# Later places for the chunk operations of layer 2: 72 dense steps from closing to table write instead of 52

## The chip, the cores and the metric

The kernel runs as one program on one NeuronCore of a Trainium2 chip. The metric is device time in microseconds for the whole program. TensorE (PE) multiplies matrices, VectorE (DVE) and ScalarE (ACT) work elementwise, GpSimd (POOL) issues the gathers, SyncE (SP) issues the other transfers. Each engine executes its own list of instructions in order and waits for the others on semaphores.

## The reference, cut to what matters

A graph with N = 6250 nodes of 128 features and 106250 edges. Three graph convolutions, then an edge-message layer:

```python
def conv(x, W_l, b_l, W_r):
    agg = segment_sum(x[src], dst) / max(degree, 1)
    return agg @ W_l.T + b_l + x @ W_r.T
h  = relu(layernorm(x))
h1 = relu(conv(h, ...))              # layer 0 of the kernel
h2 = relu(conv(h1, ...)) + h1        # layer 1
x  = x + conv(h2, ...)               # layer 2
h  = relu(layernorm(x))
m  = silu(concat(h[src], edge_attr) @ mw1 + mb1)      # layer 3
x  = h + silu(concat(h, segment_sum(m, dst)) @ uw1 + ub1) @ uw2 + ub2 + x
```

## The kernel before, in words

Nodes are handled in 49 tiles of 128 rows (`NTILE`), and these in 13 chunks of four tiles (`NCH`; the last has one tile). The edges, sorted by destination, are split: the first 600 tiles of edges of layers 1 and 2 are summed *densely*, the rest by gathers.

**Dense steps.** Layer 2 has 490 of them (`STEPS[2]`: 10 rounds of 49). Step d multiplies the two halves of node tile d % 49 with a *unit*, 128x500 counts, and accumulates into a bank (`dense_step`, L1142, two matmuls). Units are counts that SP loads piece by piece (seven units each, a ring of three pieces) and that are cast to fp32r: six of seven by ACT, one by DVE (`turn_unit`, L560). There are seven unit buffers. An engine at step i of its list casts unit i + 4 (`TURN_AHEAD`), and a cast waits until PE has used the unit seven before.

**Blocks.** Between the steps, about every sixth, PE sums one *block* of gathered edges (`sum_block`, L1092), POOL gathers the rows for it (L844, three gathers a block, a ring of seven blocks), and DVE adds the block's sum to `acc` (L1582) and makes a later one-hot (L1572). In layer 2 the 77 blocks stand at steps 34, 39, 45 and so on up to 480. At the end of each round DVE drains the bank (L1593) and adds five groups to `acc` (L1608) at steps 2, 4, 6, 8 and 10 of the next round.

**Chunks.** A chunk of nodes *closes* when all its edges are in `acc`. `CLOSING` gives the steps: 108, 157, 205, 206, 255, 304, 334, 353, 451, 457 within the rounds, and 490, 492, 494 for the last three, behind them. These are k = 0 to 12 below. For each closed chunk the rest of layer 2 and the node part of layer 3 is done, each operation some steps behind the closing, between the dense steps of the engine that does it:

- DVE multiplies by the inverse degree (`chunk_average`, L1708) at +0; PE multiplies by the two weights (`chunk_convolve`, L1212, L1213) at +4; ACT adds the bias (`convolved`, L954, "z"); PE turns it (`chunk_turn`, L1221).
- DVE zeroes the sums (`chunk_zero`, L1715), adds the input x (`chunk_residual`, L1721), and takes mean and variance (L1724, L1729); ACT takes the deviation (`chunk_deviation`, L959); DVE makes scale and shift (`chunk_shift`, L1736, L1738); ACT normalises with four activations, one per tile (`normalised`, L967).
- PE turns that (`chunk_hn_turn`, L1230), ACT copies it (`chunk_features`, L973), DVE adds it to what is kept for the output (`chunk_keep`, L1751, L1753), PE multiplies by the message weights (`chunk_message`, L1239), DVE adds a bias (`chunk_bias`, L1745), SP writes the rows to table 3 (`write_row_table`, L607).

Each engine finds its part with `closing(i, lag)`: all chunks k with `CLOSING[k] + lag == i`. SP runs by pieces and has its own places: the load of x (`load_x`, L602) at +10, the table write at `TABLE_AT + 20`. Steps from 490 on are only an order: nothing dense is left there. Each of four kinds of PE product has one bank for all chunks but k = 11, so the same operation of the next chunk waits until ACT or DVE has read the bank. Table 3 must be written completely before layer 3 gathers from it.

Of the kernel before, what the change touches and what calls it, by code (L numbers as in the profile page):

```python
# [42 lines left out]
JC = 4  # L43
CH = JC * P
NCH = -(-NTILE // JC)
# [184 lines left out]
CLOSING = [closing_tick(c) for c in TURN]  # L230
ENDING = sum(1 for t in CLOSING if t < STEPS[2])
assert TURN[ENDING:] == [7, 8, 12] and all(t + 10 < STEPS[2] for t in CLOSING[:ENDING])
CONV_AT, ZERO_AT, TURN_AT, RESIDUAL_AT, SHIFT_AT, HN_TURN_AT, MESSAGE_AT, KEEP_AT, BIAS_AT, TABLE_AT = 4, 8, 9, 10, 12, 21, 27, 20, 28, 32


def closing(i, lag):

    return [k for k in range(NCH) if CLOSING[k] + lag == i]
# [25 lines left out]
def gnn_kernel(nc, x, src_t, src_row, dst_t, dst_first, tile_first, edge_T, WlT, bl, WrT, mw1, mb1, uw1, ub1, uw2, ub2, out):  # L264
    with ExitStack() as ctx:
# [259 lines left out]
        def chunk_at(k):  # L525
            c = TURN[k]
            return c, k % 2, JC if c < NCH - 1 else JL
# [325 lines left out]
        def _(act):  # L853
# [57 lines left out]
            for l in range(4):  # L911
                if l == 0:
                    act.wait_ge(prep, PREP_PLACES)
                    act.wait_ge(starts_ready, 1)

                    def places(k):
                        return act.value_load(place_row[0:1, k:k + 1], min_val=0, max_val=P ** BT - 1)

                    def place_of(t):
                        return act.snap(((three[t % GT // BT] >> (7 * (t % BT))) & (P - 1)).with_bounds(min_val=0, max_val=G - CW))  # L920

                    three = [places(k) for k in range(GT // BT)]
                    coming = []
                    at = place_of(0)
                    for t in range(NC):
                        g = t // GT
                        if t % GT == 0:
                            after(act, counts_out[g % 2], 16 * (g // 2))
                        act.wait_ge(tile_counted, t + 1)
                        counted = nc.scalar.copy(stage[:, g % 2, :, bass.ds(at, CW)], count_bank(t))  # L930
                        if t > 0:
                            counted._wait_ge(counts_ready, t)
                        counted.then_inc(counts_ready, 1)
                        if t % GT in PLACES_AT and g + 1 < NG:
                            coming.append(places((g + 1) * GT // BT + len(coming)))
                        if (t + 1) % GT == 0:
                            three, coming = coming, []
                        if t + 1 < NC:
                            at = place_of(t + 1)
                        normalise_chunks(t)  # L940
                        if t % GT == GT - 1:
                            act.wait_ge(counts_ready, t + 1)
                            act.dma_start(counts[g], stage[:, g % 2].rearrange("p h w -> p (h w)")).then_inc(counts_out[g % 2], 16)
                elif l == 1:
                    for d in range(TURN_AHEAD, STEPS[1]):
                        turn_step(1, d)
                elif l == 2:
                    s = st[3]

                    def convolved(k):  # L950
                        c, q, n = chunk_at(k)
                        act.wait_ge(s["z_mm"], k + 1)
                        after(act, s["turned"], k - 1)
                        nc.scalar.activation(z[:, q, 0:n * P], chunk_bank(0, k)[:, 0:n * P], ACT.Identity, bias=bcol[:, 2:3]).then_inc(s["z_ready"], 1)  # L954

                    def chunk_deviation(k):
                        c, q, n = chunk_at(k)
                        act.wait_ge(s["var_ready"], k + 1)
                        nc.scalar.activation(std[:, q, 0:n], meanvar[:, q, 0:n, 1], ACT.Sqrt, bias=eps_col[:, 0:1]).then_inc(s["std_ready"], 1)  # L959

                    def normalised(k):
                        c, q, n = chunk_at(k)
                        act.wait_ge(s["y_ready"], k + 1)
                        after(act, s["hn_turned"], k - 1)
                        after(act, s["h_added"], k - 1)
                        for j in range(n):
                            m = nc.scalar.activation(hn[:, q, j, :], kept(c, n)[:, j, :], ACT.Relu, scale=rstd[:, q, j:j + 1], bias=shift[:, q, j:j + 1])  # L967
                        m.then_inc(s["hn_ready"], 1)

                    def chunk_features(k):  # L970
                        c, q, n = chunk_at(k)
                        act.wait_ge(s["hn_turned"], k + 1)
                        nc.scalar.copy(hT[:, cols(c, n)], chunk_bank(2, k)[:, 0:n * P]).then_inc(s["hT_ready"], 1)  # L973

                    for i in range(CLOSING[-1] + MESSAGE_AT):
                        if i + TURN_AHEAD < STEPS[2]:
                            turn_step(2, i + TURN_AHEAD)
                        for k in closing(i, CONV_AT):
                            convolved(k)
                        for k in closing(i, RESIDUAL_AT):  # L980
                            chunk_deviation(k)
                        for k in closing(i, SHIFT_AT):
                            normalised(k)
                        for k in closing(i, HN_TURN_AT):
                            chunk_features(k)
                elif l == 3:
                    def node_share(c):
                        n = JC if c < NCH - 1 else JL
                        act.wait_ge(st[4]["z_mm"], c + 1)
                        nc.scalar.copy(hT[:, cols(c, n)], bank[2][:, 0:n * P]).then_inc(st[4]["z_ready"], 1)  # L990

                    def last_high_half(c):

                        n = JC if c < NCH - 1 else JL
                        act.wait_ge(st[2]["high_ready"], NCH + c + 1)
                        nc.scalar.copy(last_halves[:, c * JC:c * JC + n, 0, :], hn[:, c % 2, 0:n]).then_inc(st[2]["half0_ready"], 1)

                    def updated(c):

                        act.wait_ge(st[4]["z_added"], c + 1)  # L1000
                        to = hT[:, cols(c, JC if c < NCH - 1 else JL)]
                        nc.scalar.activation(to, to, ACT.Silu, bias=bcol[:, 3:4]).then_inc(st[4]["z_ready"], 1)

                    act.wait_ge(flag_ready, 1)
                    n_left = act.value_load(left_flag[0:1, 0:1], min_val=0, max_val=EP)
                    with act.If(n_left > 0):
                        s = lf[3]
                        with act.Fori(0, NT) as t:
                            act.wait_ge(s["pre"], t + 1)
                            nc.scalar.activation(msg_left, pre_left, ACT.Silu).then_inc(s["msg"], 1)  # L1010
                    act.wait_ge(unit_used, unit_number(2, STEPS[2]))
                    for n in range(NB + SILU_AT):
                        if 2 <= n < NCH + 2:
                            node_share(n - 2)
                        for c in updates(n, SILU_AT):
                            updated(c)
                        if n >= NB:
                            continue
                        if n < NCH:
                            last_high_half(n)  # L1020
                        for k in fetch_starting(n + 3):
                            after(act, source_hot_ready, NTILE * (k - 1))
                            act.wait_ge(source_row_in[k % 2], 16 * (k // 2) + 16)
                            nc.scalar.copy(source_f[:, k % 2], source_row[:, k % 2]).then_inc(source_f_ready, 1)
                        for k in fetch_starting(n - COPY_AFTER):
                            act.wait_ge(fetch_summed, k + 1)
                            after(act, edge_mm, FETCHED[k - 1] + 1 if k > 0 else 0)
                            nc.scalar.copy(turned_pre[:, :], bank[7][:, 0:BT * P]).then_inc(fetch_copied, 1)
                        act.wait_ge(pre_ready, n + 1)
                        nc.scalar.activation(msg[:, n % NMSG], msg[:, n % NMSG], ACT.Silu).then_inc(msg_ready, 1)  # L1030
                if l < 2:
                    s = st[l + 1]
# [890 lines left out]
```

## Time and profile before

| what | value |
|---|---|
| median of 3 runs | 2372.09 us (2362.65 to 2381.28) |
| profiled execution | 2367.98 us, its span 2366.2 us |
| granted TensorE clock, mean | 0.947 |
| PE busy | 2075.7 us (88%) |
| POOL busy | 1655.9 us (70%) |
| DVE busy | 1468.7 us (62%) |
| ACT busy | 1136.4 us (48%) |

Busy times are sums over the whole span; the stages differ. The dense steps of layer 1 lie between 657 and 962 us of the span, those of layer 2 between 1002 and 1344 us, and layer 3 begins with its first gather at 1377 us. The granted clock is a share of 2.4 GHz; the clock has two levels, 1.2 and 2.4 GHz, so a mean between 0.5 and 1 is a mixture. "Idle before" in a row is the time that the engine did nothing ahead of the instruction, with what ended it behind the arrow.

### The profile page before, as it was taken

What the parts mean: (1) busy time and instruction counts of PE and PEld (TensorE: products, weight loads), DVE (VectorE), ACT (ScalarE), POOL (GpSimd) and SP (SyncE); (2) the same over time, 40 slices, a digit from 0 to 9 for tenths busy, and PEclk for the clock granted to TensorE, in tenths of its full rate; (3) what the DMA queues carried; (4) which work ended last, traced back from release to release, by engine and by line L of the source; (5) the groups of instructions that cost most, each with busy time, mean ns of one, the idle gap of its engine ahead of it and who ended that gap; (6) DMA issues with size and microseconds to landing.
All of it is one profiled execution on the core that took longest, in us unless ns stands there. A gap on an engine that the chain in (4) does not pass through costs nothing.

```text
span 2366.2 us, 44471 instructions
## 1 busy us (share of the span) xinstructions
PE 2075.7 (88%) x13062; PEld 1633.0 (69%) x13062; DVE 1468.7 (62%) x4334; ACT 1136.4 (48%) x2077; POOL 1655.9 (70%) x1666
## 2 busy tenths in 40 slices
PE   1489999999799999899999879899989889999987
PEld 0235555444378777487777658889988888888876
DVE  8878778877533333634444457667676667676764
ACT  4777777766487777687677532111111111111111
POOL 4477777777377777577766157777777777777775
PEclk9689999999899999999999979999999999999997
DMA  4389999898588778487787544434444444444432
GB/s 124 113 284 310 294 307 308 298 298 284 184 249 278 249 246 257 121 285 245 229 250 236 167 139 121 116 109 123 123 113 118 114 123 113 114 119 117 119 108 54
DMA packets 270042, 447.23 MB, mean 189 GB/s; under 512 B 34148, under 2 KB 219815, under 8 KB 263143
## 3 DMA queue, kind: packets, MB, share of 16 engines
q1 hardware_dynamic: 206680, 267.00, 37.0%
q0 software_dynamic: 55920, 114.62, 16.8%
q10 hardware_dynamic: 7200, 62.72, 6.7%
q8 instruction: 109, 1.79, 0.3%
q14 instruction: 133, 1.09, 0.1%
HBM read 363.79 MB, written 80.42 MB: 188 GB/s over the span
## 4 chain that ended last, share of the span: by engine, by line
POOL 36%; PE 33%; issue 14%; DVE 9%; DMA 3%; ACT 2%; DVEq 1%; POOLq 0%; ACTq 0%
POOL gath L844 35%; PE bank L1142 13%; PE bank L1150 6%; PE bank L1092 4%; PE bank L1111 3%; DMA gath<-table,src_sb 3%; PE bank L1192 2%; DVE region L1627 1%; PE bank L1177 1%; PE bank L1095 1%; PE bank L1114 1%; PE bank L1212 1%; ACT shared L967 1%; PE bank L1239 1%; PE bank L1161 1%
## 5 line engine op out<-in xcount | busy, mean ns | idle before, releaser
L844 POOL DMA_INDIRECT gath<-table,src_sb x1572 | 1555.3, 989 | 499.4 <-issue 457.7
L1142 PE MATMUL bank<-unit,halves 128*128 128x500 f32 x1960 | 509.3, 407 | 17.6 <-ACT unit L560 12.5
L560 ACT CAST unit<-region 128x500 fp32r<-128x500 f16 x840 | 453.7, 606 | 106.3 <-PE bank L1142 103.2
L1030 ACT ACTIVATE msg<-msg 128x384 f32<-128x384 f32 x277 | 145.2, 524 | 733.9 <-DVE msg L1670 679.2
L1192 PE MATMUL bank<-source_hot,last_halves 128*128 128x384 f32 x2352 | 494.8, 356 | 0.0
L930 ACT CAST shared<-bank 128x490 f32 x600 | 373.8, 623 | 142.7 <-PE bank L1114 108.5
L1142 PEld LDWEIGHTS bank<-unit,halves 128*128 128x128 f32 x1960 | 362.0, 193 | 92.6 <-ACT unit L560 21.8
L1698 DVE TENSOR_SCALAR source_hot<-source_f,source_col 128x384 fp32r<-128x384 f32 x1176 | 422.6, 422 | 2.1 <-PE bank L1192 1.4
L1192 PEld LDWEIGHTS bank<-source_hot,last_halves 128*128 128x128 f32 x2352 | 414.5, 196 | 3.8 <-issue 2.9
L1582 DVE TENSOR_TENSOR acc<-acc,bank 128x31 f32 (+1 forms) x548 | 105.3, 192 | 371.3 <-PE bank L1092 254.1
L1150 PE MATMUL bank<-region,parts 128*128 128x500 f16 x1176 | 318.1, 378 | 10.1 <-DVE dense_sum L1593 10.1
L1092 PEld LDWEIGHTS bank<-onehot,msg 128*128 128x128 f32 x1662 | 231.3, 201 | 135.9 <-ACT msg L1030 129.3
L1092 PE MATMUL bank<-onehot,msg 128*128 128x31 f32 x1662 | 230.2, 276 | 95.4 <-ACT msg L1030 83.5
L1670 DVE TENSOR_TENSOR msg<-bank,gath 128x384 f32<-128x384 f32 x253 | 140.5, 555 | 245.9 <-issue 166.4
L1177 PE MATMUL bank<-mw,region 128*128 128x128 f32 x1518 | 242.5, 299 | 0.9 <-DVE shared L1745 0.9
L1111 PE MATMUL bank<-region 128*128 128x490 bf16 x600 | 220.2, 395 | 20.6 <-DVE region L1627 13.0
L1627 DVE TENSOR_SCALAR region<-iota_h,key 128x540 bf16<-128x540 f16 x600 | 216.0, 395 | 28.2 <-PE bank L1114 25.3
L1177 PEld LDWEIGHTS bank<-mw,region 128*128 128x128 f32 x1518 | 203.0, 203 | 7.0 <-issue 7.0
L1150 PEld LDWEIGHTS bank<-region,parts 128*128 128x128 bf16 x1176 | 90.9, 100 | 90.9 <-issue 13.0
L1092 PEld LDWEIGHTS bank<-onehot,gath 128*128 128x128 f32 x924 | 124.4, 191 | 38.4 <-issue 29.2
L1572 DVE TENSOR_TENSOR onehot<-iota_f,rel 128x93 f32<-128x93 f32 x548 | 136.5, 251 | 0.3 <-issue 0.2
L1111 PEld LDWEIGHTS bank<-region 128*128 128x128 bf16 x600 | 59.2, 99 | 106.1 <-DVE region L1627 27.7
(164 smaller groups left out, 1686.6 us busy)
## 6 DMA issues: line engine op xcount, KB each, us to landing
region<-counts SPq DMA_DIRECT2D x196, 875.0 KB
counts<-shared ACTq DMA_DIRECT2D x50, 1225.0 KB
region<-in_edge_T SPq DMA_DIRECT2D x138, 384.0 KB
gath<-table,src_sb POOLq DMA_INDIRECT x1572
table<-shared SPq DMA_DIRECT2D x36, 256.0 KB, 2.3
table<-parts SPq DMA_DIRECT2D x12, 384.0 KB, 2.6
source_row<-in_src_row SPq DMA_DIRECT2D x24, 192.0 KB, 3.7
acc<-in_x SPq DMA_DIRECT2D x12, 256.0 KB, 5.1
```

The source lines that it names most:

```text
L560: copy(units[h][:, :].rearrange("p (b n) -> p b n", b=RG), ring[:, q, :, h * G:(h + 1) * G]).then_inc(done, 1)
L844: pool.indirect_dma_start(out=(gath if l > 0 else gath_parts)[:, BT * place + j, :], out_offset=None, in_=table[l], in_offset=bass.Indirec ...
L930: counted = nc.scalar.copy(stage[:, g % 2, :, bass.ds(at, CW)], count_bank(t))
L1030: nc.scalar.activation(msg[:, n % NMSG], msg[:, n % NMSG], ACT.Silu).then_inc(msg_ready, 1)
L1092: mm = nc.tensor.matmul(summed_in(l, n)[:, 0:W], of, onehot[:, n % HOTS, j, :], start=(j == 0), stop=(j == BT - 1))
L1111: mm = nc.tensor.matmul(count_bank(t), low_of(t), pairhot[:, t % NPAIR, 0:KW].rearrange("p (h w) -> p h w", h=NTILE), start=True, stop=(t ...
L1142: mm = nc.tensor.matmul(sum_bank(ordinal), halves[:, hi, a, :], units[h][:, :], start=(hi == 0 and a == 0), stop=(hi == NTILE - 1 and a == 1))
L1150: mm = nc.tensor.matmul(sum_bank(ordinal)[:, 0:g * G].rearrange("p (b n) -> p b n", b=g), parts[:, hi, a, :], ring[:, q, 0:g, h * G:(h + 1 ...
L1177: mm = nc.tensor.matmul(edge_bank(n)[:, j * D:(j + 1) * D], efT[:, h % NEF, t * P:(t + 1) * P], mw[:, 1, :], start=True, stop=True)
L1192: mm = nc.tensor.matmul(bank[7][:, 0:BT * P], last_halves[:, h, a, :], source_hot[:, y % NHOT, :], start=(h == 0 and a == 0), stop=False)
L1627: nc.vector.tensor_scalar(pairhot[:, t % NPAIR, :], iota_h[:, :], key[:, t:t + 1], None, ALU.is_equal).then_inc(pairhot_ready, 1)
L1698: nc.vector.tensor_scalar(source_hot[:, y % NHOT, :], source_f[:, k % 2], source_col[:, h:h + 1], None, ALU.is_equal).then_inc(source_hot_ ...
```

## The change

The lags of the chunk operations in layer 2 are set anew, in steps behind the closing:

| operation | engine | before | after |
|---|---|---|---|
| average | DVE | 0 | 0 |
| convolve | PE | 4 | 4 |
| z | ACT | 4 | 8 |
| zero | DVE | 8 | 10 |
| turn | PE | 9 | 13 |
| residual, mean and variance | DVE | 10 | 15 |
| deviation | ACT | 10 | 21 |
| shift | DVE | 12 | 24 |
| normalise, tiles 0 and 1 | ACT | 12 | 27 |
| normalise, tiles 2 and 3 | ACT | 12 | 30 |
| second turn | PE | 21 | 36 |
| keep | DVE | 20 | 36 |
| feature copy | ACT | 21 | 40 |
| message | PE | 27 | 46 |
| bias | DVE | 28 | 48 |
| table write | SP | 52 | 72 |

The last three chunks (k = 10 to 12) still normalise all their tiles at one place, +27. `chunk_deviation` waits, from k = 2 on, for the scale of the chunk two before, which reads the same buffer. The functions of the other engines are the same and take the new constants.

```diff
-CONV_AT, ZERO_AT, TURN_AT, RESIDUAL_AT, SHIFT_AT, HN_TURN_AT, MESSAGE_AT, KEEP_AT, BIAS_AT, TABLE_AT = 4, 8, 9, 10, 12, 21, 27, 20, 28, 32
+CONV_AT, Z_AT, ZERO_AT, TURN_AT, RESIDUAL_AT, DEVIATION_BY, SHIFT_AT, HN_AT, HN_REST_AT = 4, 8, 10, 13, 15, 21, 24, 27, 30
+HN_TURN_AT, KEEP_AT, FEATURES_BY, MESSAGE_AT, BIAS_AT, TABLE_AT = 36, 36, 40, 46, 48, 52
...
                         act.wait_ge(s["var_ready"], k + 1)
+                        if k > 1:
+                            act.wait_ge(st[0]["rstd_ready"], NCH + k - 1)
...
-                    def normalised(k):
+                    def normalised(k, tiles):
...
-                        for j in range(n):
+                        for j in tiles:
                             m = nc.scalar.activation(hn[:, q, j, :], kept(c, n)[:, j, :], ACT.Relu, scale=rstd[:, q, j:j + 1], bias=shift[:, q, j:j + 1])
-                        m.then_inc(s["hn_ready"], 1)
+                        if tiles[-1] == n - 1:
+                            m.then_inc(s["hn_ready"], 1)
...
-                    for i in range(CLOSING[-1] + MESSAGE_AT):
+                    for i in range(CLOSING[-1] + FEATURES_BY + 1):
...
-                        for k in closing(i, CONV_AT):
+                        for k in closing(i, Z_AT):
                             convolved(k)
-                        for k in closing(i, RESIDUAL_AT):
+                        for k in closing(i, DEVIATION_BY):
                             chunk_deviation(k)
-                        for k in closing(i, SHIFT_AT):
-                            normalised(k)
-                        for k in closing(i, HN_TURN_AT):
+                        for k in closing(i, HN_AT):
+                            normalised(k, range(JC // 2) if k < ENDING else range(chunk_at(k)[2]))
+                        for k in closing(i, HN_REST_AT):
+                            if k < ENDING:
+                                normalised(k, range(JC // 2, JC))
+                        for k in closing(i, FEATURES_BY):
                             chunk_features(k)
```

## Rows read from the trace of the kernel before

**Rows 1.** The page's chain of work that ended last, by engine.
```profile
POOL 36%; PE 33%; issue 14%; DVE 9%; DMA 3%; ACT 2%; DVEq 1%; POOLq 0%; ACTq 0%
```
**Rows 2.** Stretches: length; busy PE, PEld, DVE, ACT, POOL; clock, DMA share, GB/s.
```profile
657.10:962.00 304.90, 284.90 (x1443) 237.18 (x1442) 97.07 (x317) 228.38 (x423) 221.87 (x234) 0.98 0.82 256
1001.50:1343.60 342.10, 323.90 (x1643) 263.41 (x1642) 149.11 (x476) 252.04 (x490) 223.26 (x234) 0.97 0.76 237
1343.60:1377.00 33.40, 18.29 (x62) 12.10 (x61) 15.47 (x53) 7.38 (x18) 0.18 (x1) 0.68 0.34 107
...
1150.00:1155.00 5.00, 3.84 (x14) 3.15 (x14) 1.39 (x3) 4.17 (x9) 3.78 (x5) 0.66 0.65 196
```
**Rows 3.** Timeline of PE, layer 2: first and last block, two undisturbed ones.
```profile
1022.18 0.75 PE L1092 MATMUL bank<-onehot,gath 128*128 128x31 f32 x6
...
1281.65 0.75 PE L1092 MATMUL bank<-onehot,gath 128*128 128x31 f32 x6
...
1311.69 0.75 PE L1092 MATMUL bank<-onehot,gath 128*128 128x31 f32 x6
...
1337.75 0.75 PE L1092 MATMUL bank<-onehot,gath 128*128 128x31 f32 x6
```
**Rows 4.** Groups by line, PE, 1000 to 1345 us: busy, mean, idle.
```profile
L1212 PE MATMUL bank<-acc,wl 128*128 128x512 f32 x20 | 10.7, 618 | 2.6 <-DVE acc L1708 2.5
L1239 PE MATMUL bank<-mw,hT 128*128 128x128 f32 x80 | 10.6, 275 | 0.7 <-DVE shared L1745 0.7
...
L1230 PE MATMUL bank<-ident,shared 128*128 128x128 f32 x40 | 6.1, 277 | 0.0
```
**Rows 5.** Waits, 1000 to 1345 us: total us, times, longest us.
```profile
ACT shared L954 <- PE bank L1213: 28.6, 10, 3.6
...
ACT std L959 <- DVE meanvar L1729: 19.6, 8, 3.7
...
PE bank L1142 <- ACT unit L560: 12.5, 13, 1.5
DVE acc L1608 <- DVE acc L1608: 9.5, 11, 0.9
...
PE bank L1239 <- DVE shared L1745: 0.7, 1, 0.7
PE bank L1221 <- DVE acc L1721: 0.7, 1, 0.7
```
**Rows 6.** Timeline of PE: eight step matmuls after waits, and eight undisturbed.
```profile
1151.16 3.49 PE L1142 MATMUL bank<-unit,halves 128*128 128x500 f32 x8 [1.32 <-ACT unit L560]
...
1239.55 2.07 PE L1142 MATMUL bank<-unit,halves 128*128 128x500 f32 x8
```
**Rows 7.** Timeline of ACT around one chunk (k = 0).
```profile
1069.29 0.69 ACT L954 ACTIVATE shared<-bank,bcol 128x512 f32<-128x512 f32 x1 [3.08 <-PE bank L1213]
...
1075.94 1.64 ACT L967 ACTIVATE shared<-acc,shift,rstd 128x128 f32<-128x128 f32 x4
...
1077.49 4.16 ACT L560 CAST unit<-region 128x500 fp32r<-128x500 f16 x8
```
**Rows 8.** Groups by line, DVE, 1000 to 1345 us.
```profile
L1745 DVE TENSOR_TENSOR shared<-bank,mb_all 128x512 f32<-128x512 f32 x10 | 6.9, 690 | 15.4 <-PE bank L1239 15.4
...
L1715 DVE MEMSET acc<- 128x512 f32 x10 | 4.8, 485 | 3.7 <-PE bank L1213 3.2
```
**Rows 9.** Timeline behind the last dense step: PE, PE, POOL.
```profile
1349.71 2.08 PE L1212 MATMUL bank<-acc,wl 128*128 128x512 f32 x2 [5.72 <-DVE acc L1708]
...
1368.32 3.64 PE L1239 MATMUL bank<-mw,hT 128*128 128x128 f32 x16
...
1376.34 0.18 POOL L831 IOTA source_col_i<- 128x49 int32 x1 [62.25 <-DMA table<-shared]
```
**Rows 10.** Groups by line, POOL and PE, of layer 2 and of layer 1.
```profile
L844 POOL DMA_INDIRECT gath<-table,src_sb x231 | 220.7, 956 | 89.0 <-issue 64.1 <-PE bank L1092 24.9
...
L1092 PE MATMUL bank<-onehot,gath 128*128 128x31 f32 x462 | 59.7, 265 | 16.6 <-DMA gath<-table,src_sb 16.6
```

## The prediction

> **What bounds the kernel now.** I read the chain of waits first. POOL and PE share it, 36% and 33% [rows 1], POOL in the layers that gather every edge, PE in the dense ones. So layer 2 has to be judged by PE's own time. The busy times by stretch come next [rows 2]: the same 490 steps and 77 blocks take 304.9 us in layer 1, where no chunk work lies between them, and 342.1 us here. The third stretch, 33.4 us behind the last step, ends with the first gather of layer 3.
>
> How much of layer 2 is waiting? PE's timeline has the first and the last block and a quiet stretch [rows 3]. From 1281.65 to 1311.69 there are 9 blocks in 30.04 us: 3.34 us a block, and with 5.87 steps a block (446 steps for 76 blocks, by the code) 0.57 us a step. The 76 blocks from 1022.18 to 1337.75 took 315.6 us, and at the quiet rate they would take 253.7. The chunk work must also fit in: by busy time 10.7 us twice (the two weights), 10.6 for messages, 6.1 twice for turns, 44.2 in all [rows 4]. Matmuls overlap, so that is an upper bound; start to start they need about 28. Waiting is therefore between 18 and 34 us. The waits that the profile names on PE are 12.5 for units cast by ACT, 2.5 for the average (longest first), 0.7 and 0.7 for a bank not yet read [rows 4, 5], together 16.4. On top of them comes the clock: after three waits in a row eight matmuls took 3.49 us instead of 2.07 [rows 6], and the granted clock of that stretch is 0.66 [rows 2], that is, part of it at the lower of the two levels. The excess is 1.4 us, and there are three such places: about 4.3 us. With some 3 us at the edges (a wait is counted from the modelled end of a matmul) I take **24 us**.
>
> Who makes PE wait? Not DVE, mostly: ACT's casts are late. ACT's own idle time says why: 28.6 us ahead of z, up to 3.6 at a time, and 19.6 ahead of the deviation [rows 5]. ACT stands at those places before PE and DVE have got there, and nothing behind it is cast meanwhile. Then come four activations in one piece, 1.64 us [rows 7], and PE stops. ACT recovers slowly. Its casts follow each other every 0.52 us (eight in 4.16 [rows 7]), six in seven steps, 0.45 us a step against PE's 0.57, so it gains 0.12 us a step. The waits (some 5 us a chunk) and the operations (z 0.69, deviation 0.3, four activations 1.64, copy 0.6, together 3.2) need 70 steps to make good, more than the 49 between most closings. The operations alone need 27.
>
> **The change, part by part.**
>
> *z at +8, deviation at +21.* ACT at +8 has cast the unit of step +12, which needs the buffer of step +5, so PE has passed the product at +4: no wait is left for a chunk by itself. Deviation at +21 is 6 steps (3.4 us) behind the residual, whose DVE work lasts about 2. Both ACT waits go, 48 us of idle that PE never saw in full.
>
> *Four activations as two pairs at +27 and +30.* Same number of instructions; a pair is some 0.85 us, one and a half steps, against a lead of up to six units. For a chunk by itself PE should no longer stop. Of 12.5 plus the clock's 4.3 plus 2.5 at the edges (19.3 us) I leave 3, for the places where chunks overlap: k = 2 and 3, one step apart, put 3.3 us of activations into five steps, and k = 6 normalises where k = 7 takes z (step 361).
>
> The clock's part rests on rows 7. The Trainium skill ("TensorE: Matmul & The Clock Gate", Part 1) says that the lower level belongs to an engine that was idle, and that activity releases it. By that rule waits of about one microsecond between busy stretches would cost only themselves, and the sum below would be 4 us smaller; the trace here shows the drop inside such a stretch, and the measurement decides.
>
> *Average and convolve stay at 0 and +4.* The 2.5 us stay, perhaps 2: a message now lies shortly before most convolutions (+46 of a chunk that closed 49 steps earlier), which makes PE later by 0.8 while DVE has one bias more, 0.69 [rows 8].
>
> *k = 2 and 3 share banks.* Before, the second chunk's turn and message waited 0.7 each [rows 5]. They still do, the message more (1.2), since its bias now comes on DVE behind the fourth group addition. Two such waits are new. The convolve of k = 3 (step 210) needs z of k = 2, which stands at ACT's step 213, behind the cast for step 217, and that cast needs the unit of step 210 used: cast 0.52, z 0.69, passing on 0.2, 1.4 us of PE. The second turn (242) needs the copy at ACT's step 245 in the same way: 1.3 us. Nothing (if ACT is early) and 2.5 us each bound these.
>
> Left of the 24 us: 3 + 2 + 0.7 + 1.2 + 1.4 + 1.3 = 9.6. **Gain in the steps 14.4 us**; between 4 (only the waits ahead of z were the cause) and 28 (of 34, with 6 left).
>
> *Behind the last step.* Work of k = 8 and 9 now falls there: one second turn, two messages, two biases, one keep. PE is rid of 0.4 + 0.8 + 0.8 = 2.0 in the steps. The turn and the keep hide in PE's 5.72 us wait for the sums [rows 9] and behind it. DVE's bias for k = 8 and three memsets (0.49 [rows 8]) now precede the residual of k = 10, 1.2 us; the bias for k = 9 comes behind it, 0.7; the small residual of k = 12 ahead of the first shift, 0.75. Sum +2.7, net **+0.7**. Bounds: -2.0 (all hidden) and +5.6, both messages in line at the slow rate, 1.8 each (16 matmuls in 3.64 [rows 9]).
>
> *SP's queue.* Table writes move by as many steps as the bias, so SP reaches them no earlier in relation to it; loads of pieces stand behind them with some 13 steps of slack. Loads of x keep +10, and the x slot is free by then. I cost this at nothing; the slack is the cover. POOL has no step moved; its gathers take 0.96 us each plus 0.3 of issue, 289 us for 231, and it waited 24.9 us for PE [rows 10]. With 315.6 - 14 = 301 us on PE, the gathers are still ahead.
>
> Sum: -14.4 + 0.7 = about -14 on the profiled execution's 2368.0 (span 2366.2 and 1.8 around), 2354. That execution lies 4.1 under the median of 2372.1, so 2358; I say **2357**.
>
> **Rivals.**
>
> *All waits go.* PE lost more than it shows (the upper 34) and the shared banks cost little. Then gathers become the bound: PE would need 290 us against POOL's 289, as in layer 1, where PE waited 16.6 us for them [rows 10]. So at most 24 of gain and no tail: 2347. For it: ACT's idle time is twice PE's. Against: the new bank waits follow from the code. Chance 0.17.
>
> *The waits move.* The change does not do what it says because it is the bursts, not the waits ahead of z, that stop PE, and two pairs three steps apart do not let ACT refill; with the four bank waits, 4 us or so is left of the gain: 2367. For it: k = 2 and 3, and 5 to 7, hold over half of PE's waits, and they overlap still. Against: 0.12 us a step in ACT's favour. Chance 0.22.
>
> *Slower: DVE falls behind at the start of a round.* Chunks close ten steps into a round and the bias now comes at +48, so between the last group additions, each of which waits up to 0.9 for the one before [rows 5]. Message (0.8), bias (0.69) and one missed addition (0.9) would make DVE 2.4 us later where its average is already late; PE would stop at the convolve and again at the unit that DVE casts, 4.8 us for each of six closings, 29 us, more than the gain: 2372 + 29 - 14 = 2387. It decides from 2.4 us a closing. Against: PE passes the same message. Chance 0.06.
>
> **How the numbers follow.** The forecast (gain of 10 to 20) has 0.55, its own range 2351 to 2363. The range 2343 to 2372 takes in the two faster rivals and the scatter of medians, and leaves out the slower one. What a measurement of this kernel can tell from no change is about 1%, 24 us. Faster by more than that needs nearly the whole of the first rival or a lucky median, 0.17; slower needs the third with little gain, 0.04; within, 0.79.
>
> **What would show it.** ACT's idle time ahead of z and of the deviation falls from 48 us to under 10, PE's wait for ACT's units from 12.5 to about 3, and the stretch of the 490 steps from 342 to about 326 us. New waits stand at the convolve and second turn of k = 3. The stretch behind the last step grows by 2 to 3 us. I am wrong if PE waits for units as long as before (then bursts, not waits, were the cause), if the average becomes the longest wait, or if the stretch behind the last step grows by over 6 us.

## The result and the profile after

The changed kernel takes 2351.53 us (median of 6 runs, 2344.91 to 2354.52) against 2369.18 (6 runs, 2362.65 to 2381.28): ratio 0.9916, 95% interval 0.9891 to 0.9941, a gain of 18 us. 2357 was forecast, a gain of 15 against the median known then. The gain is under 1%, but its interval leaves out 1.

The profiled executions differ by 21.4 us (span 2344.8 instead of 2366.2). By stage, from the first and last matmul of the dense steps and the opening of layer 3 on POOL: up to layer 2, 2.0 us less; the 490 steps 319.1 instead of 342.0; behind them, to POOL's opening, 33.9 instead of 32.7; layer 3, 2.4 more. The first and the last figure belong to layers that the change does not touch; over the runs below layer 3 took 988 to 994 us and layer 2 began between 997 and 1006. The gain is the 22.9 us in the steps; a second profile of the changed kernel (after, again, below) has them at 321.8, a gain of 20.2.

The stretches after, columns as in [rows 2]:

```profile
999.50:1318.70 319.20, 310.77 (x1622) 259.19 (x1622) 145.65 (x472) 252.71 (x489) 223.61 (x234) 0.99 0.82 253
1318.70:1352.60 33.90, 20.13 (x86) 14.95 (x85) 17.95 (x57) 8.51 (x21) 0.04 (x1) 0.73 0.38 121
```

ACT is as busy as before (252.7 us against 252.0) in 23 us less, and the granted clock is 0.99 instead of 0.97. Both means hold a slow start that the change has no part in: the first steps, ahead of any closing, ran at the lower of the two levels, for longer in one execution than in another. These are the first steps before, after and in the second profile of the changed kernel:

```profile
1001.50:1011.00 9.50, 8.24 (x20) 6.15 (x20) 4.76 (x10) 6.58 (x13) 7.28 (x8) 0.51 0.50 156
...
999.50:1006.40 6.90, 5.74 (x13) 4.22 (x14) 4.62 (x10) 4.58 (x10) 4.31 (x5) 0.51 0.40 104
...
1001.40:1010.80 9.40, 8.22 (x19) 6.19 (x20) 4.64 (x10) 6.56 (x13) 6.21 (x7) 0.50 0.50 149
```

Behind them the granted clock is 0.98 before, 1.00 after and 0.99 in the second profile. The waits of layer 2 after, 998 to 1318 us, answering to [rows 5]:

```profile
ACT unit L561 <- PE bank L1149: 64.4, 99, 3.3
...
PE bank L1237 <- ACT hT L977: 2.4, 1, 2.4
...
PE bank L1246 <- DVE shared L1752: 1.5, 1, 1.5
PE bank L1219 <- DVE acc L1715: 1.5, 2, 0.9
PE bank L1219 <- ACT shared L955: 1.4, 1, 1.4
...
PE bank L1228 <- DVE acc L1728: 0.4, 1, 0.4
```

PE's wait for ACT's units, 12.5 us before, has gone from the list, and so have ACT's waits ahead of z (28.6) and of the deviation (19.6). ACT's idle time is now where it does no harm: it waits for PE to free unit buffers, 64.4 us (31.2 before), that is, it stands at its full lead. POOL, which waited 24.9 us for PE [rows 10], waits 4.9:

```profile
L845 POOL DMA_INDIRECT gath<-table,src_sb x231 | 221.2, 958 | 71.9 <-issue 67.0 <-PE bank L1099 4.9
```

The same chunk (k = 0) on ACT, answering to [rows 7]:

```profile
1066.56 0.61 ACT L561 CAST unit<-region 128x500 fp32r<-128x500 f16 x1 [1.44 <-PE bank L1149]
1067.07 0.68 ACT L955 ACTIVATE shared<-bank,bcol 128x512 f32<-128x512 f32 x1
...
1074.91 0.29 ACT L962 ACTIVATE std<-meanvar,eps_col 128x4 f32<-128x4 f32 x1
...
1078.24 0.88 ACT L970 ACTIVATE shared<-acc,shift,rstd 128x128 f32<-128x128 f32 x2
1079.02 1.61 ACT L561 CAST unit<-region 128x500 fp32r<-128x500 f16 x3
1080.54 0.87 ACT L970 ACTIVATE shared<-acc,shift,rstd 128x128 f32<-128x128 f32 x2
```

Nothing stands in brackets behind the chunk's operations: each finds its input there. Most of what PE still waits for is the meeting of k = 2 and 3:

```profile
1130.28 1.10 PE L1219 MATMUL bank<-acc,wl 128*128 128x512 f32 x2 [1.43 <-ACT shared L955]
1137.84 0.63 PE L1228 MATMUL bank<-ident,shared 128*128 128x128 f32 x4 [0.42 <-DVE acc L1728]
1154.43 0.63 PE L1237 MATMUL bank<-ident,shared 128*128 128x128 f32 x4 [2.40 <-ACT hT L977]
1163.33 1.13 PE L1246 MATMUL bank<-mw,hT 128*128 128x128 f32 x8 [1.49 <-DVE shared L1752]
```

These are the convolve, the turn, the second turn and the message of k = 3, each at a bank that still holds the result of k = 2.

### The profile page after: what moved, and what is told of

Same layout as the page of the kernel before. It is cut to its first block, busy times and chain, and to the rows that moved or that the text cites. A ratio compares the mean times of both kernels' runs of the same rounds, so it can differ in the third digit from the quotient of the medians.

```text
span 2344.8 us, 44491 instructions
## 1 busy us (share of the span) xinstructions
PE 2058.1 (88%) x13062; PEld 1622.2 (69%) x13062; DVE 1467.6 (63%) x4334; ACT 1137.3 (49%) x2077; POOL 1660.7 (71%) x1666
## 4 chain that ended last, share of the span: by engine, by line
POOL 37%; PE 31%; issue 15%; DVE 9%; DMA 3%; ACT 2%; DVEq 1%; POOLq 0%; ACTq 0%
POOL gath L845 37%; PE bank L1149 11%; PE bank L1157 5%; PE bank L1099 4%; DMA gath<-table,src_sb 3%; PE bank L1118 3%; PE bank L1199 2%; DVE region L1634 1%; PE bank L1184 1%; PE bank L1102 1%; PE bank L1121 1%; ACT shared L931 1%; PE bank L1219 1%; DVE msg L1677 0%; PE bank L1168 0%
## 5 line engine op out<-in xcount | busy, mean ns | idle before, releaser
L1149 PE MATMUL bank<-unit,halves 128*128 128x500 f32 x1960 | 497.2, 401 | 5.1 <-DVE unit L561 4.8
L1099 PEld LDWEIGHTS bank<-onehot,gath 128*128 128x128 f32 x924 | 124.7, 191 | 37.1 <-issue 27.9
```

Source lines behind the costliest of these rows:

```text
L1099: mm = nc.tensor.matmul(summed_in(l, n)[:, 0:W], of, onehot[:, n % HOTS, j, :], start=(j == 0), stop=(j == BT - 1))
L1149: mm = nc.tensor.matmul(sum_bank(ordinal), halves[:, hi, a, :], units[h][:, :], start=(hi == 0 and a == 0), stop=(hi == NTILE - 1 and a == 1))
```

## The experiments

Ratios are against the kernel before on the same chip, with the 95% interval. "Steps" runs from the start of the first to the start of the last matmul of the 490 steps, in one profile of each kernel; the waits are in that stretch. The two profiles of the changed kernel differ by 2.7 us, so differences in steps of about 3 us are no finding by themselves.

| kernel | median us | ratio | steps us | ACT ahead of z / deviation us | PE for ACT's units us |
|---|---|---|---|---|---|
| before | 2369.2 | 1 | 342.0 | 28.6 / 19.6 | 12.5 |
| after | 2351.5 | 0.9916 [0.9891, 0.9941] | 319.1 | 0 / 0 | 0 |
| e1, one piece | 2348.4 | 0.9915 [0.9901, 0.9930] | 319.6 | 0 / 0 | 0.8 |
| e2, z later | 2368.4 | 0.9998 [0.9988, 1.0008] | 342.2 | 1.0 / 23.9 | 13.1 |
| e3, deviation later | 2353.9 | 0.9930 [0.9908, 0.9953] | 326.6 | 28.0 / 0.2 | 0 |
| e5, pairs only | 2361.9 | 0.9974 [0.9961, 0.9987] | 336.8 | 27.9 / 19.6 | 8.3 |
| e7, wait apart | 2352.0 | 0.9936 [0.9918, 0.9954] | 323.7 | 0 / 23.8 | 1.9 |
| e8, gap only | 2356.9 | 0.9958 [0.9945, 0.9970] | 332.4 | 29.8 / 0.2 | 5.3 |
| e4, k = 3 apart | 2342.0 | 0.9899 [0.9879, 0.9919] | 315.9 | 0 / 0.4 | 0 |
| e6, and convolve at +6 | 2338.3 | 0.9877 [0.9855, 0.9900] | 311.2 | 3.9 / 0.4 | 0 |
| e9, z early | 2345.9 | 0.9911 [0.9896, 0.9926] | 320.6 | 26.6 / 0 | 0 |
| after, again | 2348.9 | 0.9916 [0.9901, 0.9932] | 321.8 | 0 / 0 | 0 |
| e6, again | 2337.8 | 0.9873 [0.9858, 0.9888] | 311.7 | 3.9 / 0.4 | 0 |

**e1_one_piece.** The pairs undone:

```diff
-                            normalised(k, range(JC // 2) if k < ENDING else range(chunk_at(k)[2]))
-                        for k in closing(i, HN_REST_AT):
-                            if k < ENDING:
-                                normalised(k, range(JC // 2, JC))
+                            normalised(k, range(chunk_at(k)[2]))
```

> The changed kernel with all four activations of a chunk in one piece at +27. Theory (places): ACT loses its time at places that it reaches too early, ahead of z and of the deviation; with those places later, a burst of 1.64 us meets a full lead, so PE's wait for ACT's units stays at 0 to 2 us and the time within 4 us of the changed kernel (2351 to 2356). Rival (bursts): the four activations in one piece stop PE, so PE's wait for units returns to 6 us or more and the time to 2360 or more.

Measured: 0.8 us of wait, and 0.9915 of the kernel before on its chip, against 0.9916 for the changed kernel (the 2348.4 us are a little under the range that was written down). At the new places the pairs bring nothing that can be measured.

**e2_z_later.** One piece, and only z with its own gap:

```diff
-... SHIFT_AT, HN_AT, HN_REST_AT = 4, 8, 10, 13, 15, 21, 24, 27, 30
-HN_TURN_AT, ... TABLE_AT = 36, 36, 40, 46, 48, 52
+... SHIFT_AT, HN_AT, HN_REST_AT = 4, 8, 12, 13, 15, 15, 17, 17, 17
+HN_TURN_AT, ... TABLE_AT = 26, 25, 26, 32, 33, 37
```

> Only the place of z is mended (+8, turn at +13); behind it all operations keep the small gaps of before, the deviation at the same step as the residual, and one piece. Places: ACT's idle time ahead of z falls from 28.6 to under 8 us, that ahead of the deviation stays near 20; PE's wait for units falls from 12.5 to about 5, the time to 2358 to 2364. Bursts: nothing is mended, 2366 or more, with 10 us or more of PE's wait.

Half of my theory failed. ACT's wait ahead of z fell from 28.6 to 1.0 us, as expected, and PE's wait for units did not fall at all (13.1), nor the time: the outcome that the rival of bursts had named. The run does not price the wait ahead of z by itself, since other waits came in: ACT's ahead of the deviation rose from 19.6 to 23.9 and ahead of the feature copy from 4.5 to 8.0, and PE waits 1.4 us at the convolve of k = 3 (e9 moves z alone). ACT at k = 0, and PE just behind:

```profile
1077.68 0.30 ACT L962 ACTIVATE std<-meanvar,eps_col 128x4 f32<-128x4 f32 x1 [2.99 <-DVE meanvar L1733]
1077.88 0.59 ACT L561 CAST unit<-region 128x500 fp32r<-128x500 f16 x1
1078.52 1.65 ACT L970 ACTIVATE shared<-acc,shift,rstd 128x128 f32<-128x128 f32 x4
```

```profile
1080.72 1.75 PE L1146 MATMUL bank<-unit,halves 128*128 128x500 f32 x6 [1.00 <-ACT unit L561]
```

Between the wait of 2.99 us and the 1.65 us of activations there is one cast.

**e3_deviation_later.** z, turn and residual at the places of before, the gaps of the changed kernel from there on, `4, 4, 8, 9, 10, 16, 19, 22, 25` and `31, 31, 35, 41, 43, 47`.

> Only the places from the deviation on are mended (six steps behind the residual, pairs three steps apart); z stays at +4, turn +9, residual +10. Places: ACT's idle time ahead of z stays near 28, that ahead of the deviation falls from 19.6 to under 4; PE's wait for units falls from 12.5 to about 4, the time to 2355 to 2362. Bursts: as the changed kernel, 2350 to 2354, with no wait for units.

The wait for units is gone though ACT waits 28.0 us ahead of z; here too the rival of bursts had the outcome. The trace shows why that wait is free:

```profile
1064.95 0.69 ACT L955 ACTIVATE shared<-bank,bcol 128x512 f32<-128x512 f32 x1 [3.08 <-PE bank L1220]
1065.54 5.70 ACT L561 CAST unit<-region 128x500 fp32r<-128x500 f16 x11
1071.14 0.30 ACT L962 ACTIVATE std<-meanvar,eps_col 128x4 f32<-128x4 f32 x1
1071.78 2.14 ACT L561 CAST unit<-region 128x500 fp32r<-128x500 f16 x4 [0.34 <-PE bank L1149]
```

Behind z there are eleven casts, 0.52 us each, and just behind the next operation of the chunk ACT waits for a free buffer again, that is, it is back at its full lead. The steps are still 7.5 us longer than in the changed kernel; 3.1 us of that are PE's waits for the average (4.6 us, against 1.5) and 1.0 the waits for units that DVE casts (2.1 against 1.1). The clock has a part in the rest: its first steps ran at the lower level for 9.4 us, against 6.9, and the granted clock was 0.51 from 1149.9 to 1156.8 us, about the second turn of k = 3.

**e5_pairs_only.** The places of before, `4, 4, 8, 9, 10, 10, 12, 12, 15` and `21, 20, 21, 27, 28, 32`, with normalising in two pairs.

> The places of before, but normalising in two pairs, at +12 and +15. Places: ACT's idle time stays at 28 and 19 us, PE's wait for units at 9 us or more, the time at 2364 to 2370. Bursts: PE's wait falls under 4 us, the time to 2360 or less.

Between the two theories: 8.3 us of wait (9 or more, or under 4, had been expected) and 0.9974. With the wait ahead of the deviation left in place, smaller bursts are worth 5 us of the steps.

Places alone fail in e2 and e3, bursts alone in e1 and e5. Read together, the wait ahead of z costs little or nothing, that ahead of the deviation most, and the burst counts only behind that wait. The theory became: PE stops where ACT waits *and* the activations stand right behind the wait. The next two tell that from "the wait ahead of the deviation costs by itself".

**e7_wait_apart.** The changed kernel with `DEVIATION_BY` 15 instead of 21.

> The changed kernel with the deviation back at the step of the residual (+15); the activations stay at +27 and +30, twelve steps away. ACT's idle time ahead of the deviation returns to about 20 us. Theory now (wait and burst together): it is the wait with the activations right behind it that empties the lead; twelve steps apart ACT makes the wait good, so PE's wait for ACT's units stays under 3 us and the time within 4 us of the changed kernel's 2350. Rival (the wait by itself): PE's wait for units returns to 6 us or more, the time to 2358 or more.

```profile
1074.78 0.30 ACT L962 ACTIVATE std<-meanvar,eps_col 128x4 f32<-128x4 f32 x1 [2.99 <-DVE meanvar L1736]
1074.99 5.19 ACT L561 CAST unit<-region 128x500 fp32r<-128x500 f16 x10
1080.08 0.88 ACT L970 ACTIVATE shared<-acc,shift,rstd 128x128 f32<-128x128 f32 x2
```

The same wait of 2.99 us as in e2, but ten casts lie between it and the first activations. ACT waits 23.8 us ahead of the deviation, more than before the change, and PE waits 1.9 us for units. The time cannot be told from that of the changed kernel (the intervals overlap); the steps are 4.6 us longer than in its first profile and 1.9 longer than in its second, so a few us for the wait by itself are not excluded. The activations are in pairs here; that pairs alone do not explain the fall to 1.9 us is seen in e5, where 8.3 were left.

**e8_gap_only.** The places of before with one gap of six steps ahead of the deviation, one piece: `4, 4, 8, 9, 10, 16, 18, 18, 18` and `27, 26, 27, 33, 34, 38`.

> The places of before with one gap put in: the deviation six steps behind the residual, everything behind it moved by six with the gaps of before, one piece, z at +4. Theory: the wait ahead of the deviation goes (19.6 us to under 4) and with it most of PE's wait for units (12.5 to under 3): 2351 to 2358, steps of layer 2 in 322 to 330 us. Rival (the later places of turn, message and bias bring the gain): 2364 or more.

The time is inside the range, the waits are not: steps 332.4, PE's wait 5.3. The wait ahead of the deviation went, and ACT now waits for the shift, two steps behind, 13.1 us, once more right ahead of the activations:

```profile
ACT shared L970 <- DVE shift L1742: 13.1, 6, 5.0
...
PE bank L1146 <- ACT unit L561: 5.3, 6, 2.6
```

It is the theory again, in a place that I had not looked at. What e3 has beyond this kernel is a gap between shift and activations, and the pairs; its steps are 5.8 us shorter and it has no wait for units. That this is the gap and not the pairs is likely by e1, but no run separates them here.

**e9_z_early.** The changed kernel with `Z_AT` 4 instead of 8.

> The changed kernel with z alone back at +4. Theory: ACT's idle time ahead of z returns to about 28 us in the steps, and nothing else changes: PE's wait for ACT's units under 1 us, steps of layer 2 at 317 to 320 us (the lock of k = 2 and 3 at the convolve may even go), a time within 4 us of the changed kernel run beside it. Rival (both waits of ACT cost, as the prediction had it): PE's wait for units at 3 us or more, 5 us or more slower than the changed kernel.

```profile
ACT unit L561 <- PE bank L1149: 40.6, 75, 2.5
ACT shared L955 <- PE bank L1220: 26.6, 10, 3.8
```

26.6 us of waiting ahead of z are back, taken out of the 64.4 us that ACT otherwise stands waiting for free buffers; the time is not worse (2345.9 against 2348.9 beside it). One thing helps it: PE's wait of 1.4 us at the convolve of k = 3 is gone, as had been thought possible, so the wait ahead of z may cost about that much.

**e4_k3_apart.** The changed kernel, and the chunk that is k = 3 begun 24 steps later:

```diff
-        return -(-BT * CLOSED[c] // (RG * GT)) * NTILE + ADD_AT[-1]
+        return -(-BT * CLOSED[c] // (RG * GT)) * NTILE + ADD_AT[-1] + 24 * (c == 2)
```

> The changed kernel with the work on chunk k = 3 begun 24 steps later (230 instead of 206), so that k = 2 and 3 no longer meet at the banks. Theory: the four waits of PE there (1.4, 0.4, 2.4 and 1.5 us in the profile of the changed kernel, 5.7 together) go and nothing takes their place: the steps of layer 2 from 319 to about 313 us, 2345 or so. Rival (the work is only moved, or k = 3 and 4, now 25 steps apart, wait instead): 2349 to 2353.

None of the four bank waits is left. A new one is there, at the convolve of k = 4, now 25 steps behind k = 3:

```profile
1162.20 1.13 PE L1219 MATMUL bank<-acc,wl 128*128 128x512 f32 x2 [0.93 <-DVE acc L1715]
```

The steps fell by 3.2 us against the first profile of the changed kernel and 5.9 against the second; 6 were expected, and the time (2342.0) is under the 2345 that was named.

**e6_apart_conv6.** As e4, with the convolve at +6, z at +10, zero at +12.

> As the kernel with k = 3 apart, and the convolve at +6 instead of +4, z at +10, zero at +12. Theory: PE's waits for the average (1.5 us in the steps) go too: steps 311 to 312 us, 2343 or so. Rival: z and the turn at +13 come too close, PE waits for z at the turn, 2346 or more.

The steps fell to 311.2 us, as expected, and no wait for an average is left in them. The time, 2338.3, is 5 us under what was expected. Chips could make part of that, so both kernels were run side by side:

**after_again** and **e6_again**, unedited.

> The changed kernel once more, beside the two others: 0.991 to 0.994 of the kernel before, steps of layer 2 at 319 us.

> The kernel with k = 3 apart and the convolve at +6 once more, beside the changed kernel: 7 to 13 us faster than it (8 us of it in the steps of layer 2). If chips and not kernels made the difference between the two earlier medians, under 4 us.

2337.8 against 2348.9 us: 11 us on one chip, 10 in the steps (311.7 against 321.8). This version beats both kernels, 0.9873 [0.9858, 0.9888] of the kernel before. Its profile shows what may bound it next:

```profile
POOL gath L845 <- PE bank L1099: 1.8, 6, 0.3
PE bank L1149 <- DVE unit L561: 1.5, 2, 1.1
PE bank L1099 <- DMA gath<-table,src_sb: 1.1, 2, 0.6
```

POOL hardly waits for PE any more, and PE waits for gathers in layer 2 (1.1 us; e7 had one such wait of 1.0, the changed kernel none). That the gathers are the next bound is a guess from these small waits.

## Why the prediction was right, step by step

**Who stopped PE.** Right in the engine: ACT's late casts. PE's wait for them went from 12.5 us to none. With it went the slow matmuls behind such waits: before, the granted clock was 0.51 in three stretches of 3.5 us (from 1150.8, 1246.4 and 1263.4 us), each at a wait for a unit, and in the first profile after it is 1.00 from 1006.4 us to the end of the steps. Wrong in one half of the reason. The prediction counted both waits of ACT as lost time ("48 us of idle"), and reckoned that waits and operations together need 70 steps to make good. e3 and e9 show that the 28.6 us ahead of z cost little or nothing: ACT came there with its lead full, and would have stood waiting for a free buffer anyway (64.4 us of such waiting fell to 40.6 in e9). What costs is a wait with the activations close behind it (e2, e5 and e8 against e7).

**The pairs.** Forecast as the step after which PE "should no longer stop"; with the new places they change nothing (e1), and only beside the old wait are they worth something (e5). The rival that called bursts the cause is half right for the kernel before and wrong for the changed one.

**The size of the waiting.** From the first to the last block after:

```profile
1018.95 0.75 PE L1099 MATMUL bank<-onehot,gath 128*128 128x31 f32 x6
...
1313.28 0.75 PE L1099 MATMUL bank<-onehot,gath 128*128 128x31 f32 x6
```

294.3 us, against 315.6 in [rows 3]. Of these 21.2 us some 2 are messages and a turn that moved behind the steps, so waiting fell by about 19, where the forecast was 14.4. Two terms share the miss. What was left is 7.2 us instead of 9.6 (below). And 7.2 and 19 make about 26 us of waiting before, an estimate, where the sum of named waits, the clock and the edges gave 24; the start-to-start bound of the same paragraph, 34, was further off. These blocks lie behind the slow start of the layer, so it has no part in the 21.2 us.

Part of the nearness of 2351.5 to 2357 is luck. The steps gave 20.2 to 22.9 us by profile, against 14.4; the profiled execution before lay 1.2 us under the later median, that after 5.0 under its own, and layer 3, which the change does not touch, took 2.4 us more. The measured median stands at the edge of the forecast's own range (2351 to 2363).

**What was to be left.** 9.6 us forecast, 7.2 found: 0 for overlapping bursts (3), 1.5 for the average (2), and for k = 2 and 3 a convolve of 1.43 (1.4), a turn of 0.42 (0.7), a second turn of 2.40 (1.3), a message of 1.49 (1.2). The two new bank waits, worked out from the order of the code and durations of casts, came where they were said. The second turn's was longer; ACT had just done both chunks' activations and had seven casts to make ahead of the copy:

```profile
1150.15 3.65 ACT L561 CAST unit<-region 128x500 fp32r<-128x500 f16 x7
1153.71 0.57 ACT L977 COPY hT<-bank 128x512 f32<-128x512 f32 x1
```

So part of the 3 us for bursts probably turned up here: with the activations in one piece, done earlier, this wait is 1.5 us (e1). Not in the list, and in both kernels, are waits for units that DVE casts (1.6 us before, 1.1 after). e4 bore the bank waits out by taking them away.

**Behind the last step.** +2.7 us forecast, +1.1 measured in the profile (33.9 against 32.7). The wait for the sums is 4.22 instead of 5.72, and the messages ran at the full rate (1.05 for eight matmuls), not the slow one:

```profile
1324.21 2.08 PE L1219 MATMUL bank<-acc,wl 128*128 128x512 f32 x2 [4.22 <-DVE acc L1715]
...
1329.20 1.05 PE L1246 MATMUL bank<-mw,hT 128*128 128x128 f32 x8
```

Other runs of nearly the same order had 30.6 to 35.6 there, and two profiles of the same kernel, e6, 35.5 and 32.4, so a difference of 1 us is no finding, and the +2.7 is neither borne out nor refuted.

**Costed at nothing.** POOL stayed ahead (its wait for PE fell from 24.9 to 4.9 us, and PE waited for no gather), and the SP queue held, in that PE and ACT nowhere waited for a piece of counts. Both as forecast. The 289 us for 231 gathers do not come out of the rows: 220.7 busy and 64.1 of issue are 284.8 [rows 10].

**The rivals.** "The waits move" and "DVE falls behind" are refuted: no wait for units is left, and the wait for the average in the steps fell from 2.5 to 1.5 us. "All waits go" was off by the meeting of k = 2 and 3. Its 2347 is a little nearer to the measured 2351.5 than the forecast of 2357 is. Its cap, the gathers, was set too tight: e6 goes under it, with 2338, and has only small waits for them (1.1 us).

**The clock.** The forecast held to the trace, where the lower level came inside a stretch with short waits. e8 shows it once more: after one wait of 1.32 us eight matmuls took 3.38 us instead of 2.07, at a granted clock of 0.56.

```profile
1145.75 3.38 PE L1146 MATMUL bank<-unit,halves 128*128 128x500 f32 x8 [1.32 <-ACT unit L561]
```

The Trainium skill ("TensorE: Matmul & The Clock Gate", Part 1) ties the lower level to an idle engine; this trace shows it after a wait of 1.32 us in an otherwise busy one, and there the slow matmuls cost another 1.3 us on top of the wait.

## What to carry to other kernels

An engine's idle time is no measure of what it costs others: ask whether it came to the wait with its lead full and has time to cast ahead again before its next long operation. In these runs such a wait cost little or nothing. Where a side chain is threaded through a loop, put distance between a wait and a long operation behind it; splitting the operation was the weaker remedy here (5 us of the steps in e5, 10 in e8 for the distance). And give two items that share banks different starting places, not only longer lags: with lags stretched, k = 2 and 3 waited at all four banks here.

## What the runs showed of the hardware that was not expected

A single wait of 1.32 us in otherwise dense matmuls was followed by eight matmuls near the lower of the two levels (e8, 3.38 us instead of 2.07, granted clock 0.56), while a wait of 1.00 us in e2 was not (six in 1.75 us, granted clock 1.00). The length of the wait does not decide it alone: in the kernel before, two waits of the same 1.32 us were followed by a granted clock of 1.00 (from 1078 and from 1188 us), and the wait of 1.43 us at the convolve of k = 3 was followed by 1.00 in the first profile of the changed kernel and by 0.55 in the second, at the same place of the program:

```profile
1130.28:1133.70 3.42, 3.42 (x12) 2.19 (x13) 0.00 (x0) 0.91 (x2) 2.73 (x3) 1.00 0.66 229
...
1133.29:1136.70 3.41, 3.41 (x5) 1.48 (x6) 0.00 (x0) 0.00 (x0) 2.50 (x4) 0.55 0.69 240
```

Which waits bring the clock down these runs do not settle.
